# Spreading a mixture's combine weights over 64 lanes: from a DRAM copy, or from single SBUF lanes

## The reference

```python
x = x + attention(layernorm(x))
h = layernorm(x)
weights, idx = gate(h)                  # 4 of 16 experts per token, times 2.5
combine = einsum('nke,nk->ne', onehot(idx), weights)        # [tokens, 16]
g, u = einsum('nh,ehm->enm', h, w_gate), einsum('nh,ehm->enm', h, w_up)
y_e = einsum('enm,emh->enh', silu(g) * u, w_down)
x = x + einsum('ne,enh->nh', combine, y_e) + shared_expert(h)
```

## Time and profile before

| | |
|---|---|
| Time, median of 3 runs | 751.98 us (751.13 to 752.63) |
| The profiled execution's own time | 752.66 us |
| Its span, first to last instruction | 750.8 us |
| Busy: PE, PEld, DVE, ACT, POOL | 93%, 76%, 67%, 71%, 61% |
| Granted TensorE clock, mean | 0.977 of full speed |
| DMA engines busy | 23.0% of 16 engines' span |
| HBM | 44.25 MB read, 4.72 MB written |

### The profile page before, as it was taken

How to read it: one execution, slowest core, us unless ns; L and a number is a source line. 1 busy time by engine, 2 the same in 40 slices (tenths; PEclk the granted TensorE clock), 3 DMA queues, 4 the chain that set the end, 5 groups by cost and what they waited for, 6 DMA issues and landing times.

```text
span 750.8 us, 19358 instructions
## 1 busy us (share of the span) xinstructions
PE 694.7 (93%) x6256; PEld 570.6 (76%) x6256; DVE 506.3 (67%) x1584; ACT 534.3 (71%) x1603; POOL 457.9 (61%) x564
## 2 busy tenths in 40 slices
PE   3778789999999999999999999999999999896977
PEld 1667668787888888787888878788878888685855
DVE  2456575868677686858676776858686776876434
ACT  3676778787877778787878778787877778653322
POOL 5233156767767675767676676767677774344533
PEclk9998899999999999999999999999999999999889
DMA  5010022140403132130403131230404131222231
GB/s 165 1 30 29 1 79 80 41 132 4 141 28 114 56 102 68 58 112 11 131 28 118 51 114 56 73 96 26 130 14 130 39 114 44 71 87 68 76 100 43
DMA packets 50883, 53.63 MB, mean 71 GB/s; under 512 B 5792, under 2 KB 32032, under 8 KB 50720
## 3 DMA queue, kind: packets, MB, share of 16 engines
q1 hardware_dynamic: 50848, 53.18, 23.0%
HBM read 44.25 MB, written 4.72 MB: 65 GB/s over the span
## 4 chain that ended last, share of the span: by engine, by line
PE 73%; ACT 9%; DVE 9%; issue 4%; DMA 3%; POOL 1%; SPq 0%; POOLq 0%; DVEq 0%; ACTq 0%
PE PS L981 11%; PE PS L914 11%; PE PS L802 11%; PE PS L840 9%; PE PS L804 9%; PE PS L803 9%; ACT probs L567 5%; PE PS L828 3%; PE PS L944 3%; PE PS L927 2%; DVE neg_max L724 2%; PE PS L978 2%; DVE tu L716 2%; DMA spread<-weights_by_expert 2%; ACT cT L519 1%
## 5 line engine op out<-in xcount | busy, mean ns | idle before, releaser
L567 ACT ACTIVATE probs<-PS,neg_max 128x96 f32<-128x96 f32 (+1 forms) x1024 | 246.4, 349 | 91.0 <-DVE neg_max L724 91.0
L448 POOL TENSOR_TENSOR gate<-gate,spread 128x512 f32<-128x512 f32 x128 | 163.5, 1277 | 178.8 <-ACT gate L519 86.3
L716 DVE SCALAR_TENSOR_TENSOR tu<-th,PS 128x512 f32<-128x512 f32 x128 | 87.5, 684 | 104.3 <-ACT th L535 70.1
L981 PE MATMUL PS<-wd,hh 128*128 128x128 f32 x1024 | 138.2, 278 | 14.4 <-DVE OUT L730 11.8
L981 PEld LDWEIGHTS PS<-wd,hh 128*128 128x128 f32 x1024 | 128.4, 194 | 21.0 <-DVE OUT L730 12.8
L724 DVE TENSOR_REDUCE neg_max<-PS 128x4 f32<-128x384 f32 (+1 forms) x256 | 122.5, 517 | 21.8 <-PE PS L840 17.0
L453 POOL TENSOR_TENSOR hh<-gate,tu 128x512 f32<-128x512 f32 x100 | 127.8, 1278 | 7.8
L802 PE MATMUL PS<-x_hi,w_hi 128*128 128x512 f32 x288 | 125.5, 436 | 0.2 <-DVE tu L716 0.2
L535 ACT ACTIVATE th<-PS 128x512 f32<-128x512 f32 x128 | 79.7, 623 | 53.6 <-PE PS L804 52.0
L804 PE MATMUL PS<-x_lo,w_hi 128*128 128x512 f32 x288 | 115.1, 400 | 0.0
L702 DVE STREAM_TRANSPOSE probsT<-probs 128x768 f32<-128x768 f32 (+1 forms) x128 | 114.5, 894 | 0.0
(11 more groups left out here) (102 smaller groups left out, 954.9 us busy)
## 6 DMA issues: line engine op xcount, KB each, us to landing
spread<-weights_by_expert SPq DMA_DIRECT2D x256, 128.0 KB, 3.0
X<-x SPq DMA_DIRECT2D x32, 256.0 KB, 3.4
OUT<-H SPq DMA_DIRECT2D x16, 256.0 KB, 2.9
out<-OUT SPq DMA_DIRECT2D x16, 256.0 KB, 2.9
ffn_stage<-w_gu SPq DMA_DIRECT2D x1, 1152.0 KB, 5.3
wd<-w_down SPq DMA_DIRECT2D x1, 512.0 KB, 6.4
weights_by_expert<-cT SPq DMA_DIRECT2D x16, 32.0 KB, 1.6
probsT<-w_att SPq DMA_DIRECT2D x1, 192.0 KB, 3.1
```

The lines of the kernel that those rows point to most:

```text
L448: tt(gate2[:, :], gate[:, k % 2, :], spread[:, k % SP_BUFS, :], ALU.mult).then_inc(s_g2, 1)
L567: ins = nc.scalar.activation(probs[:, u % 2, tt, 2 * rows + e, j0:KW], PS[:, rows, n * KW + j0:n * KW + KW], ACT.Exp, bias=neg_max[:, rows ...
L716: v_.scalar_tensor_tensor(tu[:, k % 2, :], th[:, :], 1.0, PS[:, 5, :], ALU.add, ALU.mult).then_inc(s_tu, 1)
L981: ins = mm(PS[:, 7, r], hh[:, k % 2, r], wd[:, k, :], start=(k == 0 and n == 0), stop=(k == NP - 1), skip_group_check=True)
```

## The change

`cT` gets two buffers, by the group's parity. The DRAM tensor, the DMA into it and its semaphore go. Each of the 16 spreading DMAs of a group reads one lane of `cT` in SBUF, 64 times, in place of 2 KB of DRAM. ACT's copy into `cT` waits on `s_g2` for the last product of the group two before.

```diff
-        cT = sb("cT", [E, TOK])
+        cT = sb("cT", [E, 2, TOK])
...
-        weights_t = nc.dram_tensor("weights_by_expert", (2, E, TOK), F32, kind="Internal").ap()
-
...
-        s_wt = sem("weights_by_expert_in_dram")
...
                 for e in range(2):
                     sp.dma_start(spread[M * e:M * e + M, k % SP_BUFS, :],
-                                 weights_t[g.par, 2 * k + e].partition_broadcast(M)
+                                 cT[2 * k + e:2 * k + e + 1, g.par, :].unsqueeze(1).broadcast_to([1, M, TOK])
                                  ).then_inc(s_spread[k % SP_BUFS], 16)
...
                         taken(sp, sl, CT % STEPS, WEIGHTS)
-                        sp.dma_start(weights_t[g.par], cT[:, :]).then_inc(s_wt, 16)
                         if not (g.fixed and g.n == 0):
                             sp.wait_ge(s_h, g.n * NP)
-                        sp.wait_ge(s_wt, 16 * g.n + 16)
                         for k in range(SP_BUFS):
                             spread_out(g, k)
...
-                            if not (g.fixed and g.n == 0):
-                                act.wait_ge(s_wt, 16 * g.n)
-                            copy(cT[:, :], bank[0:E, :], scale=0.5 * ROUTE_SCALE).then_inc(s_taken[side], 1)
+                            if not (g.fixed and g.n < 2):
+                                act.wait_ge(s_g2, (g.n - 1) * NP)
+                            copy(cT[:, g.par, :], bank[0:E, :], scale=0.5 * ROUTE_SCALE).then_inc(s_taken[side], 1)
```

## The result

The changed kernel takes 1,339.4 us (median of 4 runs, 1,338.6 to 1,339.9), against 752.3 us (751.1 to 753.9) before: 1.78 times, 95% interval 1.7765 to 1.7836. The forecast was slower, at 1,530 us.

The account below looks back on a forecast made before the run. PE bounds the kernel now, DMA after the change: 101.9 us to the first weights, 16 periods of 88.8 us (81.6 + 2.8 + 2.65 + 1.7), 4.7 and 1.9 us give 1529, predicted as 1,530 us; range 1,000 to 1,800.

Parts of the forecast that it names:

- What bounds the kernel now; the direction.: Loop period: PE bounds it, busy 41.3 of 41.8 us; after the change DMA does, at 88.8 us; slower, chance 0.86.
- The time of one transfer, 5.1 us: Each 128 KB spreading DMA: 64 pieces leave one lane one after another at 80 ns each, 5.1 us.
- 81.6 + 1.7: Per period: 81.6 us for 16 spreading transfers in strict order, 1.7 us for four 256 KB transfers sharing the queue.
- The restart, 2.8 + 2.65 us: Turn of a group: 2.8 us of start with an empty queue, 2.65 us for the last pair's product and hh.
- The removed hop, 6.3 us on the path: SP's wait for the 32 KB DMA to DRAM: on the path at four places, 1.57 us each, 6.3 us.
- rival 1: Spreading from a lane: no lane limit, period stays PE's, four hops come off, 746.4 us, up to 751; chance 0.14.
- A DMA that lands a little earlier or later there costs nothing.: Loop period before the change: PE busy 41.3 of 41.8 us, so a small shift in DMA landing costs nothing.
- Waits added on ACT and `cT`: ACT's copy into `cT` waits for products made a whole period earlier; two buffers hold nothing up: nothing.
- Rival 2, in between: Spreading DMAs: a lane beats one engine's rate insufficiently; 3 us each gives 992 us, 4.2 us gives 1,299; chance 0.10.
- 4, one engine: Spreading DMAs: all 64 pieces through one engine, 5.1 to 6.8 us, up to 1,960 us; within the likeliest case's 0.70.
- The clock: PE in a period: lower clock makes 41.3 us about 77, under 88.8; no charge, up to 80 us; within 0.70.
- Landing tens of us after issue: Sign of being right: `spread` for pairs 1 to 3 lands tens of us after its issue, queued.

Follow-up runs that it names:

- four-lane pair of kernels: Changed kernel, each spreading DMA reading four lanes 16 times each: lanes 0 to 3, 1,563.7 us; lanes 0, 4, 8 and 12, 753.9 us.
- experiment 5: Changed kernel, the second expert of each pair read from a lane nine further on (modulo 16): 882.9 us.
- experiment 6: Changed kernel, pairs 0 to 2 of a group issued without waiting for the last hh of the group before, pair 3 waiting as before: 1,263.8 us.
- side-by-side kernel: Changed kernel, each spreading DMA reading lanes 0 to 3, 16 times each: 1,563.7 us.
- experiment 3: Changed kernel, each spreading DMA reading all 16 lanes four times each: 752.3 us, 0.9994 of the kernel before.
- (9): Changed kernel, expert e in lane 4 (e mod 4) + e // 4, so that consecutive DMAs use four doors in turn: 860.4 us, 1.144 of the kernel before.
- 10: Changed kernel, expert e in lane 64 (e // 8) + 4 (e mod 8), no two of the 16 lanes neighbours: 856.3 us, 1.139 of the kernel before.

## Why the prediction was right, and where it was off

- **What bounds the kernel now; the direction.** Right. A lane is too slow a source, DMA takes the place of PE as the bound, and the period is 16 transfers and a restart. The four-lane pair of kernels shows that the cause is neighbouring lanes at one door, and the kernel with all 16 lanes as source (0.9985 to 1.0003 of before) shows that nothing else in the change costs more than such a measurement can tell. The period, 77 us, is below the 80 to 100 that I gave as a sign of being right.
- **The time of one transfer, 5.1 us.** This is the term that was mis-sized. It measured 4.8 us within a door and 4.5 us on average over a group, other transfers included. I had sized it by the best sustained rate of one engine, 25.7 GB/s; what counts is the rate of the door, and it was 27.2. The estimate by the Trainium skill's 27.2 GB/s a port ("SBUF — State Buffer", section "Door 1: The DMA port swizzle"), 4.8 us, was the right one for a transfer within a door; the 1,460 us that the sum made of it were still 120 too many. The rest is overlap: I took the queue to be in strict order, and experiment 5 shows that it isn't. By the measured 72.2 us for 16 transfers with all else that shares the queue (x 16 groups in experiment 6: (1262.0 - 106.6) / 16) the forecast's 81.6 + 1.7 = 83.3 us were 11.1 too many, and 16 x 11.1 = 178 us are nearly the whole miss of 191. About 5 of the 11 are the rate, 16 x (5.1 - 4.8). How the other 6 divide between overlap at the change of a door and beside the 256 KB transfers, the runs don't settle; the side-by-side kernel, which has no change of door, fits the forecast's sum, which has none either.
- **The restart, 2.8 + 2.65 us.** Right within a microsecond: the mean period of the changed kernel is (1336.8 - 106.6) / 16 = 76.9 us, 4.7 more than the 72.2 of experiment 6, where the sum had 5.45.
- **The removed hop, 6.3 us on the path.** The four places were right for the kernel before. But 6.3 us is more than taking the hop away gives: most of it goes to the slower landing and, at two places, to the wait for the last hh, which then ends last (experiment 3). Of the gain that rival 1 counted on no version here showed anything, even where the lane's limit is out of the way.
- **"A DMA that lands a little earlier or later there costs nothing."** Right for earlier: with 16 lanes as source the first product of a group comes 4.9 us after the last hh (437.66 to 442.59) where it was 5.5, and the time is the same. Wrong for later: in (9) it comes after 9.0 us, and the periods are 5 us longer. The forecast's sum didn't hang on it.
- **Waits added on ACT and `cT`.** Nothing, as forecast: neither stands on the chain.
- **Rival 2, in between, and 4, one engine.** The change isn't in between, but experiments 5, 9 and 10 are, since there two or more doors work at once. One engine is excluded by the busy share of 90%.
- **The clock.** The granted clock fell to 0.80 and PE's busy time in a period rose from 41.3 to 55 us, still under 77, so no charge was right. It is why PE's share of the span is 67% and not about half, as I had it.
- **Landing tens of us after issue.** Wrong: the median from issue to landing is 13.5 us, since SP is held at the issue itself. The waiting is in SP's queue, 37% of the chain, and would be missed by a reader who looks at landings alone.

```profile
spread<-cT SPq DMA_DIRECT2D x256, 128.0 KB, 13.5
```

## What to carry to other kernels

A broadcast in SBUF by DMA costs by the doors it reads from: 64 readings of one 2 KB lane are 128 KB through one door at 27 GB/s, whereas the copy in DRAM was read at 178 GB/s in the spreading burst. So count the bytes that leave each group of neighbouring lanes, not the bytes of the transfer, and compare with the period that must hide them. And before a hop is taken away, ask what the transfer behind it will take from its new source: here the hop was worth 1.57 us at four places, and even with 16 lanes as the source the slower landing took 1.15 of it back at the place shown.

## What the runs showed that I had not expected

- The order of lanes matters as much as their number. Reading one lane at a time, with consecutive transfers behind different doors, took 882.9 us in place of 1,339.4, and the same for four doors 860.4.
- SP is held when a queue is slow: with 4.8 us a transfer, the fourth, fifth and sixth issue take 4.8 us each where they took 0.6. What stands behind them on SP (inputs, stores) is held too.
- Four engines at one door got 25 GB/s, 16 engines 27 to 28, though each piece then takes 1.08 us and not 0.1. More readers may use the door a little better; two kernels are all there is on it.
- With the doors in turn the first product of a group came 3.6 us later, and the period grew by 5 to 6 us though PE is busy for over nine tenths of it: PE's idle time there also cost it some of its clock.
- A DMA whose source has four lanes used four of the 16 engines, whether near or apart: they are busy for 23% and 26% of the time, and the packets under 512 B fell from 5536 to 2464, by 12 for each of 256 transfers; with the lanes apart that was enough for this kernel.
